# Keys loaded piece by piece, and the first expert tile begun inside attention

## The chip, the cores and the metric

One core of a Trainium2 chip runs the whole program. Its engines are TensorE (PE in the rows: matmuls, and PEld for the loads of stationary operands), VectorE (DVE), ScalarE (ACT), GpSimd (POOL) and SyncE (SP, which here issues transfers). The metric is the device time of one execution in microseconds, the median over the runs shown.

## The reference, cut to what matters

Two batches of 2048 tokens of width 256 go through one post-norm layer.

```python
q, k, v = split(x @ qkv_w + qkv_b)            # 16 heads of 16
attn = softmax(rot(q) @ rot(k).T / 4)         # float32
x = layernorm(x + (attn @ v) @ out_w + out_b)
n = layer_norm(x, g1, be1);  x2 = x + n + (n @ mix_w + mix_b)
n = layer_norm(x2, g2, be2)
probs = softmax(n @ router_w);  topw, topi = top_k(probs, 2)   # 8 experts
y_e = silu(n @ w1[e] + b1[e]) @ w2[e] + b2[e]                  # 256 -> 1024 -> 256
out = layernorm(x + x2 + sum over the two chosen e of topw * y_e)
```

## The kernel before

The kernel projects queries, keys and values, and stores queries and keys in DRAM as three bf16 parts each. Then comes attention, in 8 groups of 512 queries (four for each batch), `attend(i, ...)`. A group has four units (quads of four heads) and 128 steps (32 for each unit). A step is one `score` (8 matmuls of 512 columns into one of three PSUM tiles `p_s`), one exponential of 128x1024 on ScalarE, and, in every second step, one `weigh` (8 matmuls, L1388, into `p_o`). Scores run three steps ahead of the exponentials. `scored` counts scores, and SyncE takes it as its clock.

The key rows of one batch stand in SBUF in four quads, and each quad is made of six pieces of 256 KB (`load_k`, L736, with K_ORDER saying which part each takes). The query rows of a unit are six transfers of 64 KB and one small (`load_q_rows`), in two buffers. After a unit, VectorE copies `p_o` out (`copy_out`, L1579), shuffles, takes the reciprocal and multiplies, and SyncE moves the heads to their places in `heads_T` with four transfers (`repack`, L984). While group i + 1 attends, the tokens of group i are routed: TensorE does the output projection (steps 14 to 20), the mixing, the router and the counts (step 118) between its scores, all in the one PSUM tile `small`; it waits for all repacked heads of the group at step 14 (`route`, L1430, `OUT_AT`). VectorE does the layer norms of it, and GpSimd sends the rows to the experts' regions.

SyncE has one order written out by hand. In the block `for q in range(UNITS)` at L1027 the second batch's keys are loaded: for each quad the next unit's queries, then six key pieces, whose waits on `scored` are all over by the time SyncE comes to them, then the repacking of the unit before the last.

Then come the experts: 71 tiles of 128 rows. For each tile TensorE transposes the rows (`turn_x`, L1488, into `p_x`, a part of `p_o`), does the first layer (`hide`, 32 matmuls, L1499) and the second (`reduce`, 16 matmuls, L1512), and ScalarE copies the transposed rows to `xT` (L1313), applies silu (L1305) and scales. The transposes run three tiles ahead of `reduce`, the first layer one tile. The last group's routing stands between the first tiles (`route_last`, `TAIL_AT`: its output projection after the second layer of tile 0). The tail's first lines on TensorE are these:

```python
pe.wait_ge(o_copied, GROUPS * UNITS + 1)
turn_x(0, 0, 0)
turn_x(0, 1, 1)
hide(0, 0, 0)
route_last(0)
turn_x(0, 2, 2)
```

Of the kernel before, what the change touches and what calls it, by code (L numbers as in the profile page):

```python
# [4 lines left out]
F32 = mybir.dt.float32  # L5
# [7 lines left out]
B, S, D = 2, 2048, 256  # L13
H, HD = 16, 16
E, F = 8, 1024
P = 128
# [4 lines left out]
QC = S // 512  # L21
# [734 lines left out]
def attend_route_experts(nc, dram, keep):  # L756
# [22 lines left out]
    with ExitStack() as stack:  # L779
# [63 lines left out]
        hT = room[:, KC * F:2 * KC * F].rearrange("p (u s n) -> p u s n", u=2, s=FC)  # L843
        w2 = room[:, at_quad:at_quad + E * FC * D].rearrange("p (e s n) -> p e s n", e=E, s=FC)
        b2 = room[:, at_probs:at_probs + E * D].rearrange("p (e n) -> p e n", e=E)
        xT_at = at_probs + E * D
        xT = room[:, xT_at:xT_at + 2 * KC * P].rearrange("p (u s n) -> p u s n", u=2, s=KC)
        y_at = xT_at + 2 * KC * P
        y = room[:, y_at:y_at + 2 * D].rearrange("p (u n) -> p u n", u=2)
        biased = room[:, y_at + 2 * D:y_at + 3 * D]  # L850
        rows_now = v_one[0][:, :, :, :].rearrange("p h a w -> p (h a w)")[:, 0:XR * ROW].rearrange("p (r n) -> p r n", r=XR)
        p_h = [p_s[u][:, 0:FC * P].rearrange("p (s n) -> p s n", s=FC) for u in range(2)]
        p_y = [p_s[2][:, u * 512:u * 512 + D] for u in range(2)]
        p_x = p_o[:, 0:KC * P].rearrange("p (s n) -> p s n", s=KC)

        loaded_q = keep["loaded_q"]
        loaded_k = keep["loaded_k"]
# [103 lines left out]
        def first_job(i):  # L961

            return (i - 1) * JOBS

        with nc.Block() as block:

            @block.sync
            def _(sp):
# [49 lines left out]
                    sp.wait_ge(scored, 2 * NG + 2 * NG + (k + 3) * (NG // 8))  # L1018
                    sp.dma_start(rows[name][:, :], dram[name].partition_broadcast(P)).then_inc(loaded_w, 16)
                load_x(0)  # L1020
                for c in range(1, QC):
                    for q in range(UNITS):
                        load_q(0, c, q, c * UNITS + q)
                        repack(c * UNITS + q - 2)
                    load_x(c)
                    keep_sum(c - 1)
                for q in range(UNITS):  # L1027
                    sp.wait_ge(scored, 2 * NG + (QC - 1) * NB + (q + 1) * NG)
                    load_q(1, 0, q, QC * UNITS + q)
                    for n in range(len(K_ORDER)):  # L1030
                        sp.wait_ge(scored, 2 * NG + (QC - 1) * NB + (q + 1) * NG + n * (NG // 8))
                        load_k(sp, dram, keep, 1, q, (n,))
                    repack(QC * UNITS + q - 2)
                load_x(QC)
                keep_sum(QC - 1)
                def load_w2(e):
# [244 lines left out]
            @block.scalar  # L1281
            def _(act):
                def exponentials(i, routed):
                    for n in range(NB):
                        act.wait_ge(scored, i * NB + scored_before(n) + 2 * NG)

                        act.wait_ge(weighed, i * NR + rounds_reading(held_before(n)) + LEAD)
                        nc.scalar.activation(probs[:, slot(n), :], p_s[n % BUFFERS][:, :], ACT.Exp  # L1288
                                             ).then_inc(exp_done, 1)
                        if routed and n == 104:  # L1290
                            router(i - 1)

                def router(i):
                    act.wait_ge(shifted, i + 1)
                    nc.scalar.activation(prob[:, :, :], logit[:, :, :], ACT.Exp).then_inc(router_exp, 1)

                def silu(i, r):

                    u = r % 2
                    e = act.value_load(keep["tile_expert"][0:1, bass.ds(i, 1)], min_val=0, max_val=E - 1)  # L1300
                    act.wait_ge(y_done, i + 1)
                    for fc in range(FC):
                        if fc % (FC // 2) == 0:
                            act.wait_ge(hidden, i * 2 + 1 + fc // (FC // 2))
                        last = nc.scalar.activation(hT[:, u, fc, :], p_h[u][:, fc, :], ACT.Silu,  # L1305
                                                    bias=keep["b1"][:, bass.ds(e, 1), fc])
                        if fc % (FC // 2) == FC // 2 - 1:
                            last.then_inc(h_ready, 1)

                def copy_xT(i, r):  # L1310

                    act.wait_ge(x_turned, i + 1)
                    nc.scalar.activation(xT[:, r % 2, :, :], p_x[:, :, :], ACT.Identity).then_inc(xT_ready, 1)  # L1313

                def scale_y(i, r):

                    u = r % 2
                    act.wait_ge(y_done, i + 3)
                    if not (isinstance(i, int) and i < 2):
                        act.wait_ge(added, i * 16 - 16)  # L1320
                    nc.scalar.activation(y[:, u, :], p_y[u][:, :], ACT.Identity, scale=rows_now[:, r, D + 1:D + 2]  # L1321
                                         ).then_inc(y_scaled, 1)

                def tile(turn, r, left):

                    i = turn * XR + r
                    if left > 1:
                        silu(i + 1, (r + 1) % XR)
                    if left > 3:
                        copy_xT(i + 3, (r + 3) % XR)  # L1330
                    scale_y(i, r)

                nc.scalar.activation(spare_a[:, :], identity[:, 0:1], ACT.Exp)
                exponentials(0, False)
                for i in range(1, GROUPS):
                    exponentials(i, True)
                act.sem_inc(h_ready, 4)
                act.sem_inc(y_scaled, 2)
                act.wait_ge(planned, 1)
                copy_xT(0, 0)  # L1340
                copy_xT(1, 1)
                silu(0, 0)
                copy_xT(2, 2)
                for turn in range(TAIL_TURNS):
                    for r in range(XR):
                        tile(turn, r, TILES)
                        if turn * XR + r == ROUTER_AFTER:
                            router(LAST)
                with act.Fori(TAIL_TURNS, EARLY_TURNS - 1) as turn:
                    for r in range(XR):  # L1350
                        tile(turn, r, TILES)
                act.wait_ge(planned, 2)
                with act.Fori(EARLY_TURNS - 1, TURNS - 1) as turn:
                    for r in range(XR):
                        tile(turn, r, TILES)
                for i in range((TURNS - 1) * XR, TILES):
                    tile(TURNS - 1, i % XR, TILES - i)
                act.wait_ge(step_final, LN_SCALE_STEPS)
                for a in range(BY_ACT * GT):
                    last = nc.scalar.activation(final[:, a, :], final[:, a, :], ACT.Identity,  # L1360
                                                bias=w_final["shift"][:, a:a + 1], scale=w_final["rstd"][:, a:a + 1])
                    if a % GT == GT - 1:
                        last.then_inc(normed_act, 1)

            @block.tensor
            def _(pe):
# [89 lines left out]
                def attend(i, routed, is_last, job):  # L1456

                    for n in range(NB):
# [8 lines left out]
                            weigh(i, q, kt)  # L1467
                        if routed:
                            job = job + route(i - 1, n, job)
                    return job  # L1470

                pe.sem_inc(o_copied, 1)
                pe.sem_inc(small_read, 1)
                for n in FIRST:
                    score(0, n)
                attend(0, False, False, 0)
                pe.wait_ge(loaded_w, 16 * 9)
                pe.wait_ge(constants_ready, 8)
                for i in range(1, GROUPS - 1):
                    attend(i, True, False, first_job(i))  # L1480

                def turn_x(turn, r, i):

                    pe.wait_ge(loaded_rows[r], turn * 16 + 16)
                    if not (isinstance(i, int) and i == 0):
                        pe.wait_ge(xT_ready, i)
                    for kc in range(KC):
                        last = nc.tensor.transpose(p_x[:, kc, :], rows_now[:, r, kc * P:(kc + 1) * P], identity[:, :])  # L1488
                    last.then_inc(x_turned, 1)
# [27 lines left out]
                def tile(turn, r, left, between=None):  # L1517

                    i = turn * XR + r
                    if left > 1:  # L1520
                        hide(turn + (r + 1) // XR, (r + 1) % XR, i + 1)
                    if between:
                        between(2 * i + 1)
                    if left > 3:
# [1 line left out]
                    reduce(r, i)  # L1526
                    if between:
                        between(2 * i + 2)

                job = attend(LAST, True, True, first_job(LAST))  # L1530
                routed_job = [job]
# [5 lines left out]

                pe.wait_ge(planned, 1)
                pe.sem_inc(y_done, 2)
                pe.wait_ge(o_copied, GROUPS * UNITS + 1)  # L1540
                turn_x(0, 0, 0)
                turn_x(0, 1, 1)
                hide(0, 0, 0)
                route_last(0)
                turn_x(0, 2, 2)
                pe.wait_ge(loaded_w2, 16 * E)
                for lap in range(TAIL_TURNS):
                    for r in range(XR):
# [12 lines left out]
            def _(dve):  # L1561
# [151 lines left out]
                route(LAST - 1, steps, job, True)  # L1713
                job = Job(first_job(GROUPS))
                steps = Chain(dve, step, LAST * STEPS)
                copy_out(LAST, UNITS - 1)
                route(LAST, steps, job, False)
                plan_rest(nc, dve, making, carry, keep, scratch, ended, planned)
# [161 lines left out]
```

## Time and profile before

| | us |
|---|---|
| median of 3 runs (lowest, highest) | 1686.78 (1684.42, 1687.19) |
| the profiled execution | 1684.99 |
| its span, first to last instruction | 1683.3 |
| TensorE busy in it | 1615.5 (96%) |
| ScalarE, VectorE, GpSimd busy | 1246.2, 535.5, 469.8 |
| mean granted clock of TensorE | 0.985 of full |

The span is the part that the trace shows; 1.7 us of the profiled execution's time lie around it. A busy share near 100% marks the engine that sets the pace. A stand of that engine is what can be won back, and the chain that ended last lists such stands as "issue" where the profile knows no engine that ended them, which is also so for waits on some transfers and for missing code.

### The profile page before, as it was taken

The page shows a single profiled execution, that of the slowest core. Times are in us where ns is not written, and L with a number is a line of the kernel's source. Part 1 is how long each engine was busy: PE and PEld are TensorE (multiplying, and loading weights), DVE is VectorE, ACT ScalarE, POOL GpSimd, SP SyncE. Part 2 cuts the span into 40 slices and gives each one's busy share as a digit, 9 for nine tenths or more (in the row PEclk, how much of TensorE's full clock was granted, in tenths as well). Part 3 has the DMA queues.
Part 4 walks back from the last instruction along what each step waited for, and adds up shares of the span by engine and source line. Part 5 has one row for each costly group of instructions (what it writes and reads, how often), then busy time and mean ns, then how long its engine had stood idle before and what let it go on. Part 6 is the DMA issues. An engine that isn't in the chain of part 4 may idle for free.

```text
span 1683.3 us, 45804 instructions
## 1 busy us (share of the span) xinstructions
PE 1615.5 (96%) x17940; PEld 929.7 (55%) x17941; DVE 535.5 (32%) x1442; ACT 1246.2 (74%) x1871; POOL 469.8 (28%) x495
## 2 busy tenths in 40 slices
PE   7999999999999989999999999999999999999990
PEld 5543333433433435433433433458999999999990
DVE  4551125425525525435425535525310000000004
ACT  5649999999999989999999999963444444444441
POOL 4630001202202202112202202115455444444441
PEclk9989999999999999999999999999999999999996
DMA  4775210101101354601101100646568666566645
GB/s 164 206 157 89 60 39 15 50 24 34 49 27 31 71 78 71 135 26 34 49 24 34 49 27 30 240 132 178 161 190 223 181 187 191 182 184 186 176 117 206
DMA packets 108487, 181.18 MB, mean 108 GB/s; under 512 B 14121, under 2 KB 80361, under 8 KB 108137
## 3 DMA queue, kind: packets, MB, share of 16 engines
q1 hardware_dynamic: 95010, 160.88, 33.1%
q0 software_dynamic: 13296, 17.77, 5.7%
q8 instruction: 129, 2.11, 0.5%
q14 instruction: 52, 0.43, 0.1%
HBM read 134.07 MB, written 40.18 MB: 104 GB/s over the span
## 4 chain that ended last, share of the span: by engine, by line
PE 81%; issue 5%; ACT 5%; DMA 1%; DVE 1%; POOL 0%; POOLq 0%; ACTq 0%; DVEq 0%
PE at_s L1376 24%; PE at_po L1388 23%; PE at_s L1499 14%; PE at_s L1512 14%; ACT place L1288 4%; PE at_small L1404 4%; DMA rows_out<-place,at_v 1%; PE at_small L1397 1%; PE at_po L1488 1%; DVE cb_ln_stats L696 1%; DVE place L1728 0%; DMA place<-rows_out 0%; POOL place L1242 0%; POOL place L1247 0%; POOLq L1240 0%
## 5 line engine op out<-in xcount | busy, mean ns | idle before, releaser
L1288 ACT ACTIVATE place<-at_s 128x1024 f32<-128x1024 f32 x1024 | 956.1, 1142 | 42.2 <-PE at_s L1376 41.7
L1376 PE MATMUL at_s<-place 99*32 99x512 bf16 x8192 | 582.3, 382 | 13.9 <-ACT place L1288 6.6
L1388 PE MATMUL at_po<-place,at_v 128*32 128x512 f32 x4096 | 536.3, 594 | 0.9 <-ACT place L1288 0.9
L1376 PEld LDWEIGHTS at_s<-place 99*32 99x32 bf16 x8192 | 202.0, 95 | 481.5 <-issue 222.6
L1499 PEld LDWEIGHTS at_s<-place 128*128 128x128 f32 x2272 | 265.8, 193 | 4.2 <-issue 0.8
L1305 ACT ACTIVATE place<-at_s,b_turned 128x128 f32<-128x128 f32 x568 | 162.5, 369 | 141.1 <-PE at_s L1499 138.5
L1499 PE MATMUL at_s<-place 128*128 128x128 f32 x2272 | 266.8, 276 | 0.0
L1512 PE MATMUL at_s<-place 128*128 x1136 | 256.9, 379 | 0.5 <-ACT place L1305 0.5
L1512 PEld LDWEIGHTS at_s<-place 128*128 128x128 f32 x1136 | 210.4, 190 | 26.5 <-issue 0.7
L1388 PEld LDWEIGHTS at_po<-place,at_v 128*32 128x32 f32 x4096 | 128.8, 111 | 105.1 <-ACT place L1288 2.2
L1321 ACT ACTIVATE place<-at_s,at_v 128x256 f32<-128x256 f32 x71 | 33.7, 474 | 162.0 <-PE at_s L1512 159.7
L696 DVE BATCH_NORM_STATS2 cb_ln_stats<-place 128x6 f32<-128x256 f32 x32 | 10.6, 409 | 417.1 <-DMA place<-rows_out 417.1
L1147 POOL COPY at_v<-place 128x1024 f32<-128x1024 f32 x32 | 33.3, 1041 | 375.8 <-PE at_po L1388 374.8
L1252 POOL DMA_INDIRECT rows_out<-place,at_v x71 | 114.9, 1618 | 18.9 <-issue 18.1
L1180 POOL DMA_INDIRECT rows_in<-rt_sent_rows,rt_pos x64 | 62.8, 981 | 170.5 <-PE at_po L1388 165.0
L1585 DVE RECIPROCAL at_den<-at_den 128x512 f32<-128x512 f32 x32 | 107.3, 3353 | 1.1
L1247 POOL TENSOR_TENSOR place<-place 128x256 f32<-128x256 f32 x71 | 51.8, 730 | 180.2 <-ACT place L1321 180.0
L1242 POOL TENSOR_TENSOR place<-place,at_v 128x256 f32<-128x256 f32 x71 | 80.6, 1135 | 40.2 <-issue 40.1
L1599 DVE TENSOR_TENSOR rt_x<-at_small,rt_total 128x512 f32<-128x512 f32 x32 | 22.1, 692 | 214.8 <-PE at_small L1404 214.8
L1579 DVE COPY at_o<-at_po 128x512 f32<-128x512 f32 x32 | 22.1, 692 | 203.2 <-PE at_po L1388 183.6
L499 PE MATMUL p_qk<-place,w_qk 128*128 128x512 f32 x128 | 57.4, 594 | 0.3 <-issue 0.3
L1593 DVE COPY rt_turned<-at_small 128x512 f32<-128x512 f32 x32 | 22.1, 692 | 79.1 <-PE at_small L1397 77.7
(213 smaller groups left out, 957.3 us busy)
## 6 DMA issues: line engine op xcount, KB each, us to landing
place<-in_w SPq DMA_DIRECT2D x79, 1024.0 KB, 10.1
place<-k_parts SPq DMA_DIRECT2D x48, 256.0 KB, 6.0
place<-q_parts SPq DMA_DIRECT2D x192, 64.0 KB
at_v<-rows_in SPq DMA_DIRECT2D x71, 129.0 KB
place<-in_x SPq DMA_DIRECT2D x8, 512.0 KB, 4.5
at_heads_T<-at_o SPq DMA_DIRECT2D x128, 32.0 KB
rt_x_in<-in_x SPq DMA_DIRECT2D x8, 512.0 KB, 4.1
rows_out<-rt_total SPq DMA_DIRECT2D x8, 512.0 KB, 5.9
```

Source lines behind the costliest of these rows:

```text
L499: last = nc.tensor.matmul(p_qk[ft][:, :], w_qk[:, kc, ft, :], xT[:, g % XT, kc, :], start=(kc == 0), stop=(kc == KC - 1))
L1180: nc.gpsimd.indirect_dma_start(out=dram["rows_in"], in_=sent_rows[:, n, a, :], in_offset=None, out_offset=bass.IndirectOffsetOnAxis(ap=pos ...
L1242: nc.gpsimd.tensor_tensor(biased[:, :], b2[:, bass.ds(e, 1), :].rearrange("p o n -> p (o n)"), rows_now[:, r, D + 1:D + 2].broadcast_to([P ...
L1252: nc.gpsimd.indirect_dma_start(out=dram["rows_out"], in_=y[:, u, :], in_offset=None, out_offset=bass.IndirectOffsetOnAxis(ap=rows_now[:, r ...
L1288: nc.scalar.activation(probs[:, slot(n), :], p_s[n % BUFFERS][:, :], ACT.Exp).then_inc(exp_done, 1)
L1305: last = nc.scalar.activation(hT[:, u, fc, :], p_h[u][:, fc, :], ACT.Silu, bias=keep["b1"][:, bass.ds(e, 1), fc])
L1376: last = nc.tensor.matmul(p_s[n % BUFFERS][j:j + 32, s * 512:(s + 1) * 512], k_rows[0:ROWS_M, quad(q).start + h, kt * P + j:kt * P + j + 3 ...
L1388: last = nc.tensor.matmul(p_o[32 * h:32 * h + 32, :], v_one[q % 2][:, h, kt, :], probs[:, slot(q * NG + g), s * 512:(s + 1) * 512], start= ...
L1404: last = nc.tensor.matmul(out[j:j + 32, :], weights[:, j:j + 32], moving, start=start, stop=stop, skip_group_check=lone)
L1499: last = nc.tensor.matmul(p_h[u][:, fc, :], w1_now[slot][:, kc, fc * P:(fc + 1) * P], xT[:, u, kc, :], start=(kc == 0), stop=(kc == KC - 1))
L1512: last = nc.tensor.matmul(p_y[u][:, :], hT[:, u, fc, :], w2[:, bass.ds(e, 1), fc, :].rearrange("p o n -> p (o n)"), start=(fc == 0), stop= ...
L1585: v.reciprocal(den[:, :], den[:, :]).then_inc(den_ready, 1)
```

## The change

Two edits.

The keys: the six pieces of each quad of the second batch wait for `scored` one after another, 4 steps apart, from 8 steps after the quad's last use on. Quad 0's stand after the repacking in the third unit of group 3, quad 1's after the load of x and the store of the sums, quads 2 and 3 after a query load and a repacking of the next group.

The experts' beginning: tiles 0 and 1 are transposed in step 124 of the last group, into `small` instead of `p_o`, and one VectorE copy brings both to `xT`, which has SBUF of its own now. `hide` of tile 0 runs in step 126, ahead of the last `weigh`. Tile 2's transposes move behind `hide` of tile 1, directly ahead of tile 3's. ScalarE's first two copies are gone. The functions of TensorE are only moved up in the text.

```diff
-        xT_at = at_probs + E * D
-        xT = room[:, xT_at:xT_at + 2 * KC * P].rearrange("p (u s n) -> p u s n", u=2, s=KC)
-        y_at = xT_at + 2 * KC * P
+        xT = m.sb("ex_xT", [P, 2, KC, P], F32)
+        y_at = at_probs + E * D
+        p_x_first = small[:, :].rearrange("p (t s n) -> p t s n", t=2, s=KC)
...
-                for c in range(1, QC):
+                def load_second_k(q):
+
+                    for n in range(len(K_ORDER)):
+                        sp.wait_ge(scored, 2 * NG + (QC - 1) * NB + (q + 1) * NG + NG // 4 + n * (NG // 8))
+                        load_k(sp, dram, keep, 1, q, (n,))
+
+                for c in range(1, QC - 1):
                     for q in range(UNITS):
                         load_q(0, c, q, c * UNITS + q)
                         repack(c * UNITS + q - 2)
                     load_x(c)
                     keep_sum(c - 1)
                 for q in range(UNITS):
-                    sp.wait_ge(scored, 2 * NG + (QC - 1) * NB + (q + 1) * NG)
+                    load_q(0, QC - 1, q, (QC - 1) * UNITS + q)
+                    repack((QC - 1) * UNITS + q - 2)
+                    if q == UNITS - 2:
+                        load_second_k(0)
+                load_x(QC - 1)
+                keep_sum(QC - 2)
+                load_second_k(1)
+                for q in range(UNITS):
                     load_q(1, 0, q, QC * UNITS + q)
-                    for n in range(len(K_ORDER)):
-                        sp.wait_ge(scored, 2 * NG + (QC - 1) * NB + (q + 1) * NG + n * (NG // 8))
-                        load_k(sp, dram, keep, 1, q, (n,))
                     repack(QC * UNITS + q - 2)
+                    if q < 2:
+                        load_second_k(q + 2)
                 load_x(QC)
                 keep_sum(QC - 1)
...
-                act.sem_inc(h_ready, 4)
                 act.sem_inc(y_scaled, 2)
                 act.wait_ge(planned, 1)
-                copy_xT(0, 0)
-                copy_xT(1, 1)
                 silu(0, 0)
                 copy_xT(2, 2)
...
                         if routed:
                             job = job + route(i - 1, n, job)
+                        if is_last and n == NB - 4:
+                            pe.wait_ge(small_read, job + 1)
+                            turn_first(0)
+                            turn_first(1)
+                        if is_last and n == NB - 2:
+                            hide(0, 0, 0)
                     return job
...
+                def turn_first(r):
+
+                    pe.wait_ge(loaded_rows[r], 16)
+                    for kc in range(KC):
+                        last = nc.tensor.transpose(p_x_first[:, r, kc, :], rows_now[:, r, kc * P:(kc + 1) * P],
+                                                   identity[:, :])
+                    last.then_inc(x_turned, 1)
...
                     if left > 1:
                         hide(turn + (r + 1) // XR, (r + 1) % XR, i + 1)
+                    if isinstance(i, int) and i == 0:
+                        pe.wait_ge(o_copied, GROUPS * UNITS + 1)
+                        turn_x(0, 2, 2)
...
+                pe.sem_inc(h_ready, 4)
...
                 pe.wait_ge(planned, 1)
                 pe.sem_inc(y_done, 2)
-                pe.wait_ge(o_copied, GROUPS * UNITS + 1)
-                turn_x(0, 0, 0)
-                turn_x(0, 1, 1)
-                hide(0, 0, 0)
-                route_last(0)
-                turn_x(0, 2, 2)
...
                 steps = Chain(dve, step, LAST * STEPS)
+                dve.wait_ge(x_turned, 2)
+                v.tensor_copy(xT[:, :, :, :], p_x_first[:, :, :, :]).then_inc(xT_ready, 2)
                 copy_out(LAST, UNITS - 1)
```

## Rows read from the trace of the kernel before

**Rows 1.** Stretches: us; busy PE, PEld, DVE, ACT, POOL; granted clock; DMA share; GB/s.

```profile
485.21:610.88 125.67, 123.10 (x1756) 48.52 (x1752) 53.74 (x151) 119.79 (x130) 23.93 (x18) 1.00 0.23 48
610.88:742.10 131.22, 125.77 (x1756) 53.93 (x1752) 53.77 (x151) 120.12 (x130) 23.91 (x18) 0.99 0.45 86
742.10:866.24 124.14, 123.33 (x1756) 46.97 (x1752) 53.74 (x151) 119.66 (x129) 23.94 (x18) 1.00 0.12 37
629.31:632.72 3.41, 3.41 (x31) 2.44 (x29) 0.00 (x0) 0.76 (x1) 0.00 (x0) 0.50 0.02 5
1117.41:1120.83 3.42, 3.38 (x16) 3.42 (x17) 3.39 (x2) 0.38 (x1) 0.00 (x0) 0.50 0.82 343
```

**Rows 2.** Chain that ended last: start, us, what.

```profile
596.25 1.76 issue
...
624.48 0.86 PE at_po L1388 x8
625.34 0.43 PE at_s L1376 x8
...
695.30 1.50 issue
...
1123.25 3.57 PE at_s L1499 x32
1127.04 3.46 PE at_s L1512 x16
```

**Rows 3.** Timeline of TensorE from 625 us: start, us, [idle before].

```profile
628.92 1.60 PE L1404 MATMUL at_small<-rt_out_w,at_heads_T 128*32 128x256 f32 x14 [3.14 <-issue]
```

**Rows 4.** Timeline of SyncE, 609 to 629 us.

```profile
612.17 2.66 SPq L740 DMA_DIRECT2D place<-k_parts  x6
617.90 2.41 SPq L984 DMA_DIRECT2D at_heads_T<-at_o  x4
```

**Rows 5.** DMA in 40 slices, 625.7 to 629.7; then 1121.2 to 1125.2.

```profile
DMA  8547959499645730020101010100000000000000
...
DMA  0000000000007310004521003621000731400000
```

**Rows 6.** DMA queues, 578.7 to 594.8 us: packets, MB, share.

```profile
q1 hardware_dynamic: 980, 2.00, 89.2%
```

**Rows 7.** DMA queues, 594.8 to 599.0 us.

```profile
q8 instruction: 1, 0.02, 2.7%
```

**Rows 8.** DMA queues, 866.24 to 990.39 us (group 6).

```profile
q8 instruction: 13, 0.21, 0.7%
```

**Rows 9.** DMA queues, 648.1 to 664.2 us.

```profile
q1 hardware_dynamic: 1018, 2.04, 84.2%
q0 software_dynamic: 124, 0.36, 9.7%
```

**Rows 10.** Timeline around the end of attention, 1098 to 1132 us.

```profile
1097.60 16.76 ACT L1288 ACTIVATE place<-at_s 128x1024 f32<-128x1024 f32 x18
...
1098.07 3.99 SPq L1046 DMA_DIRECT2D at_v<-rows_in  x4
...
1112.05 0.60 PE L1376 MATMUL at_s<-place 99*32 99x512 bf16 x8
...
1114.51 1.07 PE L1388 MATMUL at_po<-place,at_v 128*32 128x512 f32 x8 [0.86 <-ACT place L1288]
...
1115.63 0.69 DVE L1579 COPY at_o<-at_po 128x512 f32<-128x512 f32 x1 [6.32 <-PE at_po L1388]
...
1116.38 0.44 PE L1488 MATMUL at_po<-identity,at_v 128*128 128x128 f32 x2 [0.80 <-DVE at_o L1579]
1116.92 0.38 ACT L1313 ACTIVATE place<-at_po 128x256 f32<-128x256 f32 x1 [2.55 <-PE at_po L1488]
...
1117.45 0.66 PE L1488 MATMUL at_po<-identity,at_v 128*128 128x128 f32 x2 [0.63 <-ACT place L1313]
...
1121.22 2.41 SPq L984 DMA_DIRECT2D at_heads_T<-at_o  x4
```

More of the change, by code:

```diff
@@ L1469, in attend @@
                             job = job + route(i - 1, n, job)
-                    return job
[L1472 to L1480, printed above, removed]
+                        if is_last and n == NB - 4:
[4 more added lines that the diff above has]
+                            hide(0, 0, 0)
+                    return job
+                def turn_first(r):
[4 more added lines that the diff above has]
+                    last.then_inc(x_turned, 1)
                 def turn_x(turn, r, i):
                     pe.wait_ge(loaded_rows[r], turn * 16 + 16)
-                    if not (isinstance(i, int) and i == 0):
-                        pe.wait_ge(xT_ready, i)
+                    pe.wait_ge(xT_ready, i)
                     for kc in range(KC):
@@ L1528, in tile @@
                         between(2 * i + 2)
+                pe.sem_inc(o_copied, 1)
+                pe.sem_inc(small_read, 1)
+                pe.sem_inc(h_ready, 4)
+                for n in FIRST:
+                    score(0, n)
+                attend(0, False, False, 0)
+                pe.wait_ge(loaded_w, 16 * 9)
+                pe.wait_ge(constants_ready, 8)
+                for i in range(1, GROUPS - 1):
+                    attend(i, True, False, first_job(i))
                 job = attend(LAST, True, True, first_job(LAST))
```

## Prediction

> **What bounds the kernel now.** I read the busy shares by stretch first. In the second batch's first undisturbed group of 512 queries TensorE works 123.33 of 124.14 us [rows 1], so attention runs at TensorE's pace and ScalarE's exponentials (119.66 us) are just under it. The two groups at the change of batch take 125.67 and 131.22 us for the same work: 1.53 + 7.08 = 8.61 us more than 2 x 124.14 [rows 1]. That is everything an edit at this place can win.
>
> The chain that ended last says where it goes: TensorE stands for 1.76 us at 596.25 and for 1.50 us at 695.30, both in the middle of a score [rows 2], and for 3.14 us ahead of the output projection at 628.92 [rows 3]. After the last one its granted clock is 0.50, the 1.2 GHz level, for 3.41 us [rows 1]; the matmuls of that stretch take twice their time, so it costs 3.41 / 2 = 1.7 us. 1.76 + 1.50 + 3.14 + 1.7 = 8.1 of the 8.6 us.
>
> Why it stands: the SyncE timeline shows six key transfers issued in one go at 612.17 and the heads' transfer (the repacking) behind them at 617.90 [rows 4]. The slices of the DMA view from 625.7 on (0.1 us each) show packets up to 628.3; TensorE starts its projection at 628.92, 0.62 us later [rows 5, 3]. So the 3.14 us are the heads, queued behind 1.5 MB of keys. The two stands in mid-score wait for no semaphore. There the transfers tell: from 578.7 to 594.8 us the view lists one queue alone, the data's 980 packets, and no instruction queue [rows 6], and in the next 4.2 us one instruction block comes [rows 7], while in a quiet group 13 blocks come in 124.15 us, one per 9.5 us [rows 8]. I read both stands as TensorE out of code, its block waiting behind a key burst. One burst (648.1 to 664.2: the two data queues alone) also kept the blocks out for 16.1 us [rows 9] and the chain has no stand there, so up to about 16 us between blocks is bearable.
>
> **Part 1, the keys.** The same 24 transfers of 256 KB are issued; none is added. Each now waits for its own step of scores, 4 steps apart, and a quad's six go behind a heads' transfer instead of ahead of one. A step is 124.14 / 128 = 0.97 us, so pieces come 3.9 us apart. A burst moved 2.00 MB in 16.1 x 0.892 = 14.4 us [rows 6], 7.2 us per MB, so a piece keeps the DMA engines for 1.9 us: half of each 3.9 us is free. A block of code then waits 2 us at most, giving 9.5 + 2 = 11.5 us between blocks, against 16.1 us that did no harm. Queued behind the new waits on SyncE are the next query load (it waits for the end of the unit anyway, 4 steps past the last piece) and the next repacking (one step range later as well), so neither is late. For the repacking of the group's last unit nothing lies ahead now but its query load; issued at 617.90 [rows 4] it takes what the last one of the kernel takes with little else in flight: that is issued at 1121.22 [rows 10] and its packets end at 1124.7 [rows 5], so 3.5 us. It would be done at 621.4, 4.4 us ahead of the 625.78 at which TensorE asked. One place is less tidy: quad 1's pieces stand behind a repacking, an x load and a store of sums, so that two or three come together, 4 to 6 us in a row. Bounds: all 8.61 us come back, or 1 to 2 us of code waits stay. I take 8.6, since 9.5 + 6 = 15.5 us is still under 16.1.
>
> By the Trainium skill, "Runtime: NRT & Kernel Launch", section "Instruction fetch mechanics", TensorE holds 2048 instructions and is refilled in blocks of 256. A block late by one place would then never be missed, and the two mid-score stands would have another cause; the sum by it is with the rivals. The trace speaks against it: both stands follow a burst without blocks and end just after one has come.
>
> **Part 2, the end of attention.** Before, step by step [rows 10, 2]: last score at 1112.05; last weighing at 1114.51; copy of the output 1115.63; tile 0's transposes 1116.38; ScalarE's copy 1116.92; tile 1's transposes 1117.45; hide(0), at clock 0.50 from 1117.41 for 3.41 us [rows 1]; hide(1) from about 1123.1; reduce(0), 3.46 us, from 1127.0; output projection of the last group from 1130.43.
>
> After, from the same 1112.05. The score is 8 matmuls, 0.43 us [rows 2]: to 1112.48. Four transposes at the pace of hide's 32 matmuls of the same shape (3.57 / 32 = 0.11 us) are 0.44 us: to 1112.92. They wait for the counts' buffer, which VectorE has read by then (it has been idle for 6.32 us at 1115.63, so since 1109.31), and for rows 0 and 1, whose six transfers are all issued by 1102.06, 10 us ahead [rows 10]. The new DVE copy of 128x512 takes the 0.69 us of the row at 1115.63, and starts 0.54 us after the second pair of transposes as ScalarE's did (1116.38 to 1116.92): 1112.70 + 0.54 + 0.69 = 1113.93. Nothing on VectorE waits behind it, since the last copy_out can't start before the last weighing. Meanwhile TensorE weighs round 14 (8 matmuls, 0.86 us [rows 2], to 1113.78); hide(0) begins at 1113.99, 0.06 us after the copy as at 1116.38, and takes 3.57 us [rows 2]: to 1117.56. Hidden under it is the last exponential, over at 1114.36 [rows 10].
>
> The last weighing thus starts at 1117.56 instead of 1114.51, 3.05 us later, and with it all that hangs on it: copy, reciprocal, repacking. TensorE goes on: weighing to 1118.42, hide(1) to 1121.99, tile 2's transposes, then tile 3's, which need ScalarE's copy between. That round trip is 1117.45 - 1116.38 = 1.07 us [rows 10]; hide(1) covered it before and nothing does now, a new stand of 0.85. Tile 3's transposes 1123.06, reduce(0) 1123.28 to 1126.74. ScalarE is no limit: it has silu(0) alone to do, which falls under hide(1).
>
> Then comes the output projection, and it needs the heads. Their packets end at 1124.7 [rows 5], TensorE could go 0.62 us later, at 1125.3, 10.8 us after the last weighing's start. Now: 1117.56 + 10.8 = 1128.4. So TensorE stands for 1.6 us, and the projection starts 1130.43 - 1128.4 = 2.0 us earlier, not 3.7. What is late next is nothing: the tiles behind it run back to back. Bounds: 3.7 (the heads come sooner) and 0.3 (the stands of 0.85 and 1.6 us bring the clock down as three of 0.86, 0.80 and 0.63 did [rows 10], costing 1.7). I take 2.1: 1.76 us alone left the clock up.
>
> The sum: 8.6 + 2.1 = 10.7 us. The profiled execution took 1684.99 us, the three runs have the median 1686.78; 1684.99 - 10.7 = 1674.3 and 1686.78 - 10.7 = 1676.1. I give the latter.
>
> **Rivals.**
> Code waits aren't the keys' doing. Then 1.76 + 1.50 = 3.3 us stay: 1679.4. For it: no row names the code as the releaser. Against: two stands, both at the end of a burst. 0.10. The Trainium skill's "DMA: Bandwidth & Descriptors", "Queues, rings and completion order", would have an engine alternate between rings after each packet, so a block would not wait out a burst; 16.1 us without one [rows 6, 9] disagree.
> The change doesn't space the pieces: SyncE is held by what stands ahead (quad 1), the burst comes back in part and one code wait of 1.6 us stays: 1677.7. 0.10.
> The clock falls at the new stands at the end: 1676.1 + 1.7 = 1677.8. 0.08.
> Slower: every block now meets a piece. The pieces stretch over 116 steps, 113 us, in which 12 blocks come; should each leave TensorE standing for the 1.63 us of the two stands' mean, it is 19.6 us: 1695.7. It decides from 10.7 / 12 = 0.9 us per block on. Against it is the burst of 16.1 us that cost nothing. 0.04.
> As forecast: 0.63. The last 0.05 is for code that shifts so that blocks fall elsewhere, with about no change.
>
> **How the numbers follow.** This kernel's runs agree within 2.8 us, so 0.2% (3.4 us) is about what can be told from no change. Faster by more: 0.88; within: 0.08; slower: 0.04. The range reaches down to 1672.5 (all of 3.7 at the end, and the runs' own scatter) and up to 1680.5 (the code rival with scatter).
>
> **What would show it.** Right: groups 3 and 4 at 124 to 125 us each; no stand at the projection of group 3; clock 1.00 through both places; the last group's projection about 2 us nearer its last score, with a wait of 1 to 2 us on a transfer ahead of it; hide(0) in 3.57 us. Wrong: mid-score stands of over 1 us among the pieces, or a projection wait of over 3 us at the end with the clock at 0.50.

## The result and the profile after

The changed kernel takes 1675.87 us (median of 4, 1675.38 to 1677.22) against 1686.21 (median of 4) of the kernel before: ratio 0.9947, interval [0.9935, 0.9959]. 1676.1 was forecast. The profiled execution took 1675.51 us, its span is 1673.8.

Groups 3, 4 and 5 in the busy times by stretch (columns as in [rows 1]):

```profile
485.45:609.62 124.17, 123.36 (x1756) 46.34 (x1752) 53.82 (x151) 119.69 (x130) 23.92 (x18) 1.00 0.36 74
609.62:733.78 124.16, 123.35 (x1756) 46.35 (x1752) 53.83 (x151) 119.69 (x129) 23.88 (x18) 1.00 0.26 65
733.78:857.95 124.17, 123.36 (x1756) 46.33 (x1752) 53.83 (x151) 119.69 (x129) 23.90 (x18) 1.00 0.13 37
```

The 8.6 us of [rows 1] are all back: 125.67 + 131.22 - 124.17 - 124.16 = 8.56, and the granted clock stays at 1.00. SyncE's timeline has the heads ahead of the keys now, and TensorE's has no idle time noted before the projection:

```profile
616.65 2.42 SPq L984 DMA_DIRECT2D at_heads_T<-at_o  x4
619.11 8.36 SPq L740 DMA_DIRECT2D place<-k_parts  x4
```

```profile
624.35 1.03 PE L1413 MATMUL at_small<-rt_out_w,at_heads_T 128*32 128x256 f32 x16
```

The DMA view of 609.62 to 733.78 us has the instruction blocks at the rate of a quiet group (13 in [rows 8]):

```profile
q8 instruction: 14, 0.23, 0.8%
```

That q8 is the queue of TensorE's code is read from the counts: its blocks are of 16 KB (0.23 MB / 14), and over four groups of this trace (489.5 to 986.2 us) 55 of them came while TensorE ran 14020 matmuls and weight loads, one block for 255.

At the end of attention the chain that ended last reads so:

```profile
1105.98 3.77 PE at_s L1511 x32
1109.75 1.00 PE at_po L1397 x8
1110.74 3.77 PE at_s L1511 x32
1114.51 0.23 PE at_po L1500 x2
...
1115.30 0.41 PE at_po L1500 x2
1115.70 0.54 issue
1116.25 3.71 PE at_s L1524 x16
1119.96 0.86 issue
1120.83 1.93 PE at_small L1413 x32
```

And the timeline, where what ended each stand is named:

```profile
1103.79 0.61 PE L1385 MATMUL at_s<-place 99*32 99x512 bf16 x8
...
1109.68 1.07 PE L1397 MATMUL at_po<-place,at_v 128*32 128x512 f32 x8
...
1115.30 0.41 PE L1500 MATMUL at_po<-identity,at_v 128*128 128x128 f32 x2 [0.56 <-ACT ex_xT L1325]
...
1116.42 2.93 SPq L984 DMA_DIRECT2D at_heads_T<-at_o  x4
```

From the last score's start to the last group's projection it is 1120.83 - 1103.79 = 17.04 us; before it was 1130.43 - 1112.05 = 18.38 [rows 10]. So 1.3 us came from here in this pair of traces. The further traces of the old order below, which take 16.77 us, show that this was not the change's doing.

### The profile page after: what moved, and what is told of

The parts are those of the page before. It is cut to its first block, busy times and chain, and to the rows that moved or that the text cites. A ratio compares the mean times of both kernels' runs of the same rounds, so it can differ in the third digit from the quotient of the medians.

```text
span 1673.8 us, 45794 instructions
## 1 busy us (share of the span) xinstructions
PE 1610.3 (96%) x17936; PEld 916.9 (55%) x17941; DVE 536.7 (32%) x1443; ACT 1244.0 (74%) x1869; POOL 469.3 (28%) x495
## 4 chain that ended last, share of the span: by engine, by line
PE 81%; ACT 4%; issue 4%; DVE 1%; DMA 1%; POOL 0%; POOLq 0%; ACTq 0%; DVEq 0%
PE at_s L1385 24%; PE at_po L1397 23%; PE at_s L1511 14%; PE at_s L1524 14%; ACT place L1300 4%; PE at_small L1413 4%; PE at_small L1406 1%; PE at_po L1500 1%; DMA rows_out<-place,at_v 1%; DVE cb_ln_stats L696 1%; DVE place L1750 0%; POOL place L1254 0%; DMA place<-rows_out 0%; POOL place L1259 0%; DVE at_v L1714 0%
## 5 line engine op out<-in xcount | busy, mean ns | idle before, releaser
L1385 PE MATMUL at_s<-place 99*32 99x512 bf16 x8192 | 575.3, 381 | 12.7 <-ACT place L1300 7.6
L1385 PEld LDWEIGHTS at_s<-place 99*32 99x32 bf16 x8192 | 195.0, 95 | 485.6 <-issue 220.2
L1511 PEld LDWEIGHTS at_s<-ex_xT,place 128*128 128x128 f32 x2272 | 264.3, 192 | 5.9 <-issue 1.7
L1511 PE MATMUL at_s<-ex_xT,place 128*128 128x128 f32 x2272 | 265.7, 275 | 0.0
L1524 PEld LDWEIGHTS at_s<-place 128*128 128x128 f32 x1136 | 210.4, 190 | 27.3 <-issue 1.6
L1397 PEld LDWEIGHTS at_po<-place,at_v 128*32 128x32 f32 x4096 | 125.3, 111 | 104.4 <-issue 1.2
```

Of the source, the lines that this page charges most:

```text
L1385: last = nc.tensor.matmul(p_s[n % BUFFERS][j:j + 32, s * 512:(s + 1) * 512], k_rows[0:ROWS_M, quad(q).start + h, kt * P + j:kt * P + j + 3 ...
L1397: last = nc.tensor.matmul(p_o[32 * h:32 * h + 32, :], v_one[q % 2][:, h, kt, :], probs[:, slot(q * NG + g), s * 512:(s + 1) * 512], start= ...
L1511: last = nc.tensor.matmul(p_h[u][:, fc, :], w1_now[slot][:, kc, fc * P:(fc + 1) * P], xT[:, u, kc, :], start=(kc == 0), stop=(kc == KC - 1))
L1524: last = nc.tensor.matmul(p_y[u][:, :], hT[:, u, fc, :], w2[:, bass.ds(e, 1), fc, :].rearrange("p o n -> p (o n)"), start=(fc == 0), stop= ...
```

## Experiments

"Last score to projection" below is always that stretch, read from TensorE's timeline; it is the figure that the expert half can move. The rest of the program varies between traces without regard to the change: the starts of group 3 lie up to 1.9 us apart, and what follows the projection's start takes 552.5 to 553.3 us.

**The keys alone** (the kernel before, with the SyncE part of the diff only).

> The keys' half of the change alone on the kernel before. My theory (the heads queued behind a burst, and code blocks queued behind bursts): groups 3 and 4 both take 124.1 to 124.3 us, no stand of over 0.5 us in them, the clock stays at 1.00 there; 8.3 to 8.6 us below the kernel before, ratio 0.995. Rival (code waits not the keys' doing): 5.3 us only, with stands of about 1.5 us left in mid-score. Rival (the two halves need each other): under 4 us.

Measured: 1675.48 us (5 runs) against 1684.52 (29 runs of the kernel before), ratio 0.9952 [0.9939, 0.9965]: the changed kernel's time. Groups 3 and 4 take 124.18 and 124.15 us, at clock 1.00.

The surprise is its end of attention, which nothing changed:

```profile
1103.75 0.60 PE L1388 MATMUL at_s<-place 99*32 99x512 bf16 x8
...
1106.21 1.07 PE L1400 MATMUL at_po<-place,at_v 128*32 128x512 f32 x8 [0.86 <-ACT place L1300]
1108.08 0.44 PE L1500 MATMUL at_po<-identity,at_v 128*128 128x128 f32 x2 [0.81 <-DVE at_o L1591]
...
1109.39 3.74 PE L1511 MATMUL at_s<-place 128*128 128x128 f32 x32
...
1120.52 0.85 PE L1416 MATMUL at_small<-rt_out_w,at_heads_T 128*32 128x256 f32 x11
```

The three stands (the third, not shown, is 0.63 us) are those of [rows 10] to 0.01 us, but hide(0) takes 3.74 us, where in the first trace of the kernel before it took 5.13 us, most of it at half the clock, and the stretch is 16.77 us, less than the changed kernel's 17.04.

**The expert half alone** (the changed kernel with the SyncE part of before).

> The expert half alone, keys as in the kernel before. My theory: the last score to the last group's output projection takes 17.0 us as in the changed kernel, against 18.4 before, so 1.3 us below the kernel before (ratio 0.999, hardly to be told from none by the times), and groups 3 and 4 still take 125.7 and 131.2 us. Rival (the expert half works only because the keys' half calms the transfers): 18 us or more from the last score to the projection. Rival (it saves more than the span between shows, further on): 2.5 us or more below.

Measured: 1685.92 us (12 runs), ratio 1.0005 [0.9994, 1.0017]. Groups 3 and 4 take 125.52 and 131.41 us. Last score to projection 17.61 us, with a wait of 1.46 us for the heads (SyncE took 3.49 us for their four issues). No gain can be measured.

**The kernel before, and the keys alone, once more**, for second traces.

> The kernel before once more, for a second trace. My theory (the slow-clock stretch at the end of attention depends on how the stands fall and is no fixed cost): groups 3 and 4 lose 7 to 10 us again; the three stands at the end are again 0.86, 0.80 and 0.63 us; the clock may or may not fall there, and the last score to the projection of the last group takes 18.4 us with the fall and about 16.7 without. Rival (the fall is a fixed property of this order of work): the clock falls again.

> The keys' half alone once more, for a second trace. Its first trace had the stands at the end of attention without a fall of the clock. My theory: the last exponential's end to the last group's projection takes 14.5 us without a fall, 16.1 with one; groups 3 and 4 take 124.2 us each. Rival (the fall at the end was a fixed cost of the order before, and the first trace an exception): 16.1 us.

Measured: 1686.86 and 1676.19 us, one run each. Groups 3 and 4 of the kernel before lose 10.4 us this time (126.14 and 132.52), with the clock down in two places there (0.56 over the 3.5 us behind the stands that end at 630.46 and 698.77). At its end the three stands are again 0.86, 0.81 and 0.63, and behind them, in the busy times by stretch:

```profile
1121.15:1124.56 3.41, 3.41 (x33) 3.41 (x32) 3.38 (x2) 1.67 (x2) 0.00 (x0) 1.00 0.74 303
```

Clock 1.00. Last score (1115.51) to projection (1132.28) is 16.77 us, and 16.77 in the keys-only kernel as well. So the old order takes 16.77 us in three traces of four, and 18.38 in the one that the prediction read: the 1.6 us between are the fall of the clock (half of the 3.41 us at 0.50 [rows 1] is 1.7).

**The pieces in one burst, but behind the heads.**

```diff
-  sp.wait_ge(scored, ... + (q + 1) * NG + NG // 4 + n * (NG // 8))
+  sp.wait_ge(scored, ... + (q + 1) * NG + NG // 4)
```

> The changed kernel with the six pieces of a quad issued in one go, but still behind the heads' transfers. This parts the order from the spacing. My theory of two causes: the 3.1 us stand at the output projection of group 3 is gone (order), but instruction blocks are shut out for 15 to 18 us at each burst and one to three mid-score stands of about 1.5 us each come back: 1.5 to 4.5 us above the changed kernel. Rival (the order is everything): the same time as the changed kernel within 0.5 us. Rival (the spacing is everything, the heads were late because the engines were busy): a stand of 2 to 3 us at the projection returns as well, 5 us or more above.

Measured: 1684.57 us (10 runs), ratio to before 1.0 [0.999, 1.001]; groups 3 and 4 take 127.70 and 129.16 us. More is lost than I expected (8.7 us above the changed kernel, not 1.5 to 4.5), with the heads in time. TensorE in order of time:

```profile
579.52 0.61 PE L1385 MATMUL at_s<-place 99*32 99x512 bf16 x7 [2.27 <-issue]
...
639.37 0.41 PE L1413 MATMUL at_small<-rt_out_w,at_heads_T 128*32 128x256 f32 x2 [2.82 <-issue]
```

The projection starts 627.74 - 613.01 = 14.7 us into its group, as in the changed kernel (624.35 - 609.62), so the heads were there. But mid-work stands of 2.27, 0.94 (at 607.95) and 2.82 us came (the last inside the projection's matmuls, which had begun and so had their data), and the clock fell after the last (0.61 over 639.37 to 642.80). The queues that the DMA view lists from 618.2 to 636.4 us:

```profile
q1 hardware_dynamic: 604, 1.70, 67.7%
q0 software_dynamic: 117, 0.34, 10.1%
q14 instruction: 1, 0.01, 0.4%
```

No q8 block for 18.2 us. Both rivals fall: the order is not everything, since nothing is won without the spacing, and the heads were not late for busy engines. What the spacing is worth in the old order was not tried.

**Pieces 2 steps apart** (NG // 16 for NG // 8).

> The changed kernel with pieces 2 steps (1.94 us) apart instead of 4. A piece keeps the transfer engines for about 1.9 us, so they are as busy as in a burst while the six go, but only one or two pieces are queued at any time. My theory (a block waits for what is queued ahead of it, not for busy engines): blocks at most 13 us apart, no stand, the same time as the changed kernel within 1 us. Rival (busy engines starve the blocks whatever the queue): blocks 15 us or more apart and stands as with bursts, 1.5 to 4.5 us above.

Measured: 1679.99 us (10 runs), ratio 0.9973 [0.9963, 0.9983]; 4.1 us above the changed kernel. My theory missed. There were stands of 1.94 us, ending at 580.50, and of 0.77 us, ending at 637.40. The list from 565.5 to 577.2 us bears on the first:

```profile
q1 hardware_dynamic: 838, 1.91, 104.6%
q14 instruction: 1, 0.01, 0.6%
```

A piece takes as long as the spacing, so the transfer engines had data queued without a break, and no block came in 11.7 us. The block before, at 565.4, had itself come 12.9 us after its predecessor: two late ones in a row were enough, at gaps far under the 16.1 us of [rows 9]. The second stand follows a gap of 16.3 us.

**Extra bursts in quiet groups**, first as stores of key rows to an unused DRAM tensor, then as real key loads (a quad loaded again with the same data; six, six, six, six, then five, four, three, two pieces, each behind a heads' transfer).

```diff
+  for n in range(pieces):
+      sp.dma_start(dram["kept"][...], keep["place"][n * HD:(n + 1) * HD, 0:2 * S]...)
```

> The changed kernel with extra bursts in two quiet groups (key rows stored to a DRAM tensor that nothing reads, 256 KB a transfer in 4096-byte rows): six in each unit of group 5, then five, four, three and two in those of group 6, each burst behind a heads' transfer. The computation is otherwise the same. My theory (instruction blocks queue behind bursts): blocks are shut out for 15 us or more at bursts of six, with at least one mid-score stand of over 0.5 us in group 5; at bursts of three and two blocks are at most 13 us apart and nothing stands; no heads' wait anywhere. Rival (it takes the writes to 16 partitions, or the heads): no gap over 13 us and no stand in either group.

```diff
+  load_k(sp, dram, keep, 1, (q - 2) % UNITS, range(RELOADED[c - 1][q]))
```

> The changed kernel, with key quads loaded a second time, with the same data, in quiet groups: the real key transfers, so 4096-byte packets into 16 partitions. Each time the pieces go in one burst behind a heads' transfer: four bursts of six, then bursts of five, four, three and two. My theory (an instruction block is not served while its transfer engine has key packets queued, so what matters is how long a burst keeps the queues filled without a break): blocks 14 us or more apart at several bursts of six, at least one mid-score stand of over 0.5 us among the four, and at the bursts of three and two no gap over 13 us and no stand. Rival (it was the stores and other loads at the change of batch): no gap over 13 us and no stand, as with the stores to DRAM in the run before, which moved 16384-byte packets.

The stores did nothing in their groups: both take 124.2 us, and no two blocks are more than 13 us apart there. The time, 1677.44 us, is of a single run whose trace is 1.3 us behind the changed kernel's before the first store. A block comes in the middle of a burst of six (745 to 755 us):

```profile
q1 hardware_dynamic: 239, 1.62, 92.2%
...
q8 instruction: 1, 0.02, 0.8%
```

The loads did: 1680.23 us (a single run), and group 5 takes 128.03 us. TensorE after the second and the fourth burst of six:

```profile
761.18 0.40 PE L1394 MATMUL at_s<-place 99*32 99x512 bf16 x3 [0.79 <-issue]
...
828.07 0.21 PE L1422 MATMUL at_small<-rt_router_w,rt_turned 128*32 128x8 f32 x4 [2.63 <-issue]
```

The lists around the fourth burst, 807.1 to 825.5 us:

```profile
q1 hardware_dynamic: 884, 1.99, 80.5%
q14 instruction: 1, 0.01, 0.4%
```

The first two bursts of six left 15.2 and 15.5 us between blocks. Behind the bursts of five, four, three and two nothing stood. So real key bursts make the mid-work stands in a group where neither heads nor a change of batch is near. One thing doesn't fit: during the third burst of six (778.7 to 790.8 us) two blocks came through:

```profile
q1 hardware_dynamic: 478, 1.57, 89.8%
...
q8 instruction: 2, 0.03, 1.9%
```

**Where in the program the stands fall.** The blocks leave a mark that can be counted. Between the two mid-score stands of the kernel before lie 1274 matmuls and 1274 weight loads:

```profile
597.50:696.20 98.70, 93.33 (x1274) 43.14 (x1274) 42.83 (x118) 88.17 (x94) 17.16 (x14) 0.98 0.50 80
```

With the 12 semaphore instructions of TensorE that the trace has there as well, and the view leaves out, it is 2560 = 10 x 256. The same count gives 768 and 768 between the three stands of the burst behind the heads, 1536 between the two of the half spacing and 1792 between the two of the reloads. All 13 mid-work stands of over 0.5 us in groups 3 to 6 (six of this case's traces have such stands) are whole multiples of 256 instructions apart, and each ends 2.5 to 3.4 us after a q8 block began. So they stand at the borders of blocks, waiting for code.

The wait ahead of group 3's projection does not: it begins 755 instructions after the first stand, 13 short of a border, at the projection's first matmul, and it has the same place in the other two traces with the old order of the keys (2.51 and 3.63 us there). That fits a wait for the heads. But the block for that border began only at 625.07. TensorE passed it at 629.24. Even with the heads in time it would have stood there until about 627.6 to 628.4 (an estimate from the 2.5 to 3.4 us above), so the late heads alone cost some 0.8 to 1.6 us. This goes far to explain why the order alone won nothing.

**The register read ahead of the wait** (TensorE's read of tile 0's expert number moved ahead of tile 3's transposes).

> The changed kernel with TensorE's read of tile 0's expert number ahead of the wait for tile 3's transposes instead of behind it. My theory (the 0.54 us idle ahead of the second layer of tile 0 is that read, laid bare because the wait before it is no longer covered; and the heads decide the projection): the 0.54 us go to under 0.1, the wait at the projection grows from 0.86 to about 1.4 us, the time is the same within 0.3 us. Rival (TensorE's own work decides the projection): 0.5 us below. Rival (the idle time is the wait for silu): it stays 0.5 us.

Measured: 1676.45 us (5 runs), the same within scatter. TensorE:

```profile
1103.43 0.60 PE L1385 MATMUL at_s<-place 99*32 99x512 bf16 x8
...
1115.18 3.71 PE L1527 MATMUL at_s<-place 128*128 x16
1120.40 0.85 PE L1413 MATMUL at_small<-rt_out_w,at_heads_T 128*32 128x256 f32 x12 [1.51 <-issue]
```

The 0.54 us ahead of the second layer are gone (so they were the read, not the wait for silu), the wait for the heads has grown from 0.86 to 1.51, and the stretch is 16.97 us. The heads decide.

**The last weighing first** (hide(0) behind the last weighing, tile 2's transposes between hide(0) and hide(1), both as before the change; tiles 0 and 1 still transposed in step 124).

```diff
-                        if is_last and n == NB - 2:
-                            hide(0, 0, 0)
...
                 pe.sem_inc(y_done, 2)
+                hide(0, 0, 0)
+                pe.wait_ge(o_copied, GROUPS * UNITS + 1)
+                turn_x(0, 2, 2)
```

> The changed kernel with the first layer of tile 0 behind the last weighing (as before the change) and tile 2's transposes between the first layers of tiles 0 and 1 (as before), but tiles 0 and 1 still transposed in step 124. My theory (the last group's output projection starts 11.1 us after the last weighing starts, or when TensorE is through, whichever is later): the last weighing starts 2.5 us after the last score instead of 5.9, the heads are there 13.3 to 13.6 us after it, TensorE is through at 14.8 to 15.2 without the round trip and without the 0.54 us ahead of the second layer, no wait at the projection; 1.8 to 2.3 us below the changed kernel. Rival (moving the first layer into attention is what the change gains by): 1 us or more above the changed kernel.

> The weigh-first kernel once more, as the best version so far, on the chip of the run beside it. My theory: 14.7 us from the last score to the projection, groups 3 and 4 at 124.2 us each, about 1672.5 us, ratio to the kernel before 0.993. Rival (the first measurement was luck): 1675 us or more.

Measured: 1672.52 us (6 runs), ratio 0.993 [0.9916, 0.9945], and 1672.65 (5 runs), 0.9927 [0.9913, 0.994]. It beats both kernels; the kernel with the register read early, measured beside the first, took 1676.45. In the first one's timeline:

```profile
1103.57 0.60 PE L1385 MATMUL at_s<-place 99*32 99x512 bf16 x8
...
1106.02 1.06 PE L1397 MATMUL at_po<-place,at_v 128*32 128x512 f32 x8 [0.27 <-ACT place L1300]
...
1118.25 1.07 PE L1413 MATMUL at_small<-rt_out_w,at_heads_T 128*32 128x256 f32 x16
```

14.68 us from the last score (14.82 in the second), with one stand of 0.27 us.

**Only the last weighing first** (as above, but tile 2's transposes stay behind hide(1)).

> As the weigh-first kernel, but tile 2's transposes stay behind the first layer of tile 1, as in the change. This parts the two things that the weigh-first kernel undid. My theory: the last weighing starts 2.4 us after the last score starts; the round trip to ScalarE (0.57) and the register read (0.54) stand bare again, so the last score to the last group's projection takes 14.7 + 1.1 = 15.8 us, with no wait for the heads: 1.1 us above the weigh-first kernel and 1.3 us below the changed one. Rival (the gain of weigh-first is all the round trip's): 17.0 us, as in the changed kernel.

Measured: 1674.69 us (4 runs), ratio 0.9936 [0.9921, 0.9952].

```profile
1103.42 0.60 PE L1385 MATMUL at_s<-place 99*32 99x512 bf16 x8
...
1115.07 0.41 PE L1498 MATMUL at_po<-identity,at_v 128*128 128x128 f32 x2 [0.57 <-ACT ex_xT L1325]
1116.00 3.28 PE L1522 MATMUL at_s<-place 128*128 x14 [0.51 <-issue]
```

The projection starts at 1119.64: 16.22 us, 0.4 more than I had said; its two stands are 1.08 us of the difference to 14.68. It lies between: 0.8 us below the changed kernel's 17.04 for the weighing, 1.5 above 14.68 for the round trip.

## Why the prediction was right, and where it was not

The sign and most of the gain were right by part 1. That the time came within 0.3 us of 1676.1 is in part luck. The sum took off 8.6 + 2.1 from 1686.78, the median of three runs, where 29 later runs of the same kernel have the median 1684.52 (other sets 1684.01 of 12 and 1686.10 of 9). The 2.1 us that part 2 did not bring are about what the start was above the median of the 29: from there the keys' 8.6 alone give 1675.9.

The terms of part 1, one by one:

- Group 3 and 4 give back all 8.61 us: 8.56 measured, and 9.0 with the keys' half alone (1684.52 to 1675.48), which is the whole gain.
- The heads queued behind the keys: the wait was theirs, and with the heads ahead it is gone even if the burst stays. But the term of 3.14 us was put down to them whole, and by the estimate above half of it or more was the same late code as at the other stands, hidden behind their wait: the 18.7 us without a block from 606.3 to 625.1 are the longest gap in that trace's change of batch. The burst behind the heads only showed it elsewhere, as 2.82 us.
- The two mid-score stands as late code: right. The real key loads in quiet groups show that bursts cause such stands, with no q8 block in the 18.4 us ahead of the one at 828.07, and their places, 256 instructions or a multiple of it apart, show that it is code that TensorE waits for.
- "Up to about 16 us between blocks is bearable" was wrong as a rule. The half-spaced pieces had a stand after 11.7 us without a block, the one before that being late too. The change holds not because of a threshold but because its queues run dry between pieces. The late blocks are also worth more than the 3.3 us that I set: with bursts behind the heads their stands, 6.0 us in all, and what follows them (the fall of the clock among it) eat the whole gain.

The step that failed is part 2, "the projection starts 1130.43 - 1128.4 = 2.0 us earlier". The half is worth nothing: 1675.87 with it, 1675.48 without it, and 17.04 us against 16.77 from the last score to the projection. Two terms were mis-sized.

- The old order's stretch. I took 18.38 us from one trace and had the fall of the clock in it as a fixed cost. In three further traces with the same three stands it did not fall: 16.77 us. I priced a fall as a rival for the new order and never asked whether the old one always has it.
- The new order's stretch. I worked out 1128.37 - 1112.05 = 16.3 us; it is 17.04. The last weighing starts 5.89 us after the last score, not 5.51, and the heads are there 11.15 us after it, not 10.8 (SyncE took 2.93 us for the four issues, where it had taken 2.41). Both are small, and both lie on the path that I had named: with the register read out of the way the stretch was 16.97 us, the same but for 0.07.

The new stands were forecast as 0.85 and 1.6 us. The round trip showed as 0.56 us, and 0.54 behind it that I had not seen; 0.86 was left for the heads, since TensorE came there later: 1.96 us in all, against 2.30 before. The change replaces three stands by three others. What it gets wrong is the order. The last weighing starts 5.89 us after the last score instead of 2.46, since hide(0) (3.77 us) goes ahead of it. Nothing urgent waits for hide(0), and the chain that the projection waits for (copy, reciprocal, repacking; 11.15 us) waits for the weighing. With the weighing first, and tile 2's transposes back in their old place, the early transposes of tiles 0 and 1 give 16.77 - 14.68 = 2.1 us, or 1.95 in the second trace. The medians of both measurements lie some 3 us below those of the changed and the keys-only kernel. The rest of it lies outside this stretch, and no run tells what it is.

By the Trainium skill, "DMA: Bandwidth & Descriptors", "Queues, rings and completion order", an engine alternates between its rings after each packet. The bursts of stores and one burst of loads agree; most other key bursts don't, with 14.5 to 19.0 us without a block where 9.3 are usual.

Open: why key loads keep the blocks out and stores do not, and why blocks came through the third burst of six and not through the others. Also that the fall of the clock at the end of attention happens in one trace of four: no run here tells what decides it.

## What to carry to other kernels

Space bulk loads so that the queue runs dry in between; a spacing equal to the transfer's own time is no spacing. Put a transfer that someone waits for ahead of them, but do not expect that alone to help: here a second wait stood behind the first. When stands have no named releaser, count the engine's instructions between them: a common multiple points to code that comes in blocks. When work is pulled forward into a stage's last steps, ask which instruction there starts the longest chain, and let that one go first. Take a fall of the clock out of a stretch before comparing it, or look at a second trace: one trace can hold a cost that the next has not.

## What had not been expected of the hardware

- Six loads of 256 KB, each into 16 partitions, mostly left 14.5 to 19.0 us between TensorE's instruction blocks, and the stands that follow reach 2.8 us with no engine named in the profile. Six stores of the same size left no more than 13 us.
- A block began about 9 us before TensorE reached its first instruction when nothing held it up, so about one block ahead; where it began only 2.5 to 3.4 us before, TensorE had stood.
- Runs of the kernels with such bursts seem to scatter more: 1680.3 to 1689.3 us over 29 runs of the kernel before and 1679.6 to 1686.4 over 10 with the burst behind the heads, while each of the six kernels with the pieces 4 steps apart, at 4 to 6 runs each, stays within 2.7 us. Part of this is the number of runs: the four of the result for the kernel before span 2.8 us.
- The read of a register's value on TensorE, right behind a wait that no queued work covered, cost 0.51 to 0.54 us in three traces, and nothing where it was moved ahead of that wait.
- The same three stands of 0.86, 0.81 and 0.63 us were followed by a granted clock of 0.50 once and of 1.00 three times.
